# Feed-forward input, shifted by one token: built by two SyncE transfers instead of two ScalarE copies

## The chip, the cores and the metric

The kernel runs on one core of a Trainium2 chip. The metric is the device time of one execution in microseconds (us).

## What is computed

A block of four parts: attention with L2-normalised rows, a transformer of depth 6 on 8 sequences of 256 tokens by 128 features, attention with relative positions, and a mixture of 8 experts. Most of the time goes to the transformer. Each of its six layers is:

```python
def shift_tokens(t):
    a, s = jnp.split(t, 2, -1)
    s = jnp.pad(s, ((0, 0), (1, 0), (0, 0)))[:, :-1]
    return jnp.concatenate([a, s], -1)
for i in range(DEPTH):
    x = attn_layer(shift_tokens(x), Wqkv[i], q_scale[i], k_scale[i], Wo[i]) + x
    x = ffn_layer(shift_tokens(x), ln_g[i], ln_b[i], W1[i], b1[i], W2[i], b2[i]) + x
```

The shift leaves the first 64 features where they are and moves the other 64 one token later. `attn_layer` is attention in windows of 32 tokens with 16 heads of 64; `ffn_layer` is a layer norm over the features, a gated product with GELU, and a projection back.

## The kernel before, in words

The stream `Z` lies in SBUF with features on the 128 partitions and tokens on the free axis, one [128, 256] slab for each of the 8 sequences. A layer of one sequence is an item: 48 items, `t = layer * 8 + sequence`. Every engine has its own program, written out in order, and engines meet at counting semaphores. Each of them calls `step(t, ...)`, and a step has eight slots `s`. In step `t` three items are at work: item `t` has its projections, norms and rotation, item `i = t - 1` its attention, item `f = t - 2` its output projection and feed-forward part. Step `t` therefore holds the shifted input of item `t - 2`.

What happens at the start of a step, around that input:

- TensorE ends the output projection of `f` (`project_out`, L593). VectorE adds it to `Z` (`add_attention`, L1261) and raises `z1_done`.
- ScalarE, slot 0, in order: square and copy of the projection (L901, L904), two copies of a turned key block (L929, L930), then the two copies of the shifted input (L975 for the 64 features that stay, L976 for the 64 that move), a values copy (`take_values`, L915, raises `v_done`), the turned probabilities (L942). The second xf copy raises `xf_ready`.
- TensorE, slot 1, in order: projection of the next block (L512), the mean of `xf` over the features as a matmul with a constant matrix (`ln_mean_pe`, L395), which waits for `xf_ready` and `z_ready`; then the turn of the last block of item `i` (L523), its second weighing (L572), a turn of its output (L581), the variance (L401), values (L533).
- VectorE, slot 1, begins with the subtraction `xf - mean` (`ln_d_dve`, L1113, raises `ln_d`); ScalarE squares that (L854). Normalisation, norms (L1225 to L1219), the division of the weighed values (L1250, L1254) and the rotation (L1234) follow.
- `xf` is one buffer. Partition rows 64 to 127 of its token 0 are zeroed once (L1128).

SyncE issues DMAs in the order of its own program (`layer`). For item `t`: `spread_values(t, 0)`, `load_xs(t + 1)`, `spread_values(t, 1)`, `spread_values(t, 2)`, `spread_values(t, 3)`. `load_xs` makes the shifted input of the attention part by two transfers from Z (L325, L326, 64 KB and 63.8 KB). `spread_values(t, j)` waits for `v_done >= 8 t + 2 j + 2` and then issues four transfers (two for the last group) of 130 KB inside the values tile `vp` (L335). The copy that completes group 2 of item `t` is the values copy of ScalarE in slot 0 of step `t + 1`, the one right behind the two xf copies. Between these stand, at the first, second and last item of a layer, the loads of the next weights.

The waits that matter, in TensorE's slot 1 and in ScalarE's slot 0:

```python
                    if s == 1 and p2:
                        pe.wait_ge(xf_ready, f + 1)

                        pe.wait_ge(z_ready, B + f)
                        ln_mean_pe(xf[:, :], S, LN_S2 + f, bank[3])
```

Of the kernel before, what the change touches and what calls it, by code (L numbers as in the profile page):

```python
# [20 lines left out]
P = 128  # L21
B, S, DIM, H = 8, 256, 128, 16
TOK = B * S
DEPTH = 6
ITEMS = DEPTH * B
# [56 lines left out]
def build(nc, a, out):  # L82
    ctx = ExitStack()
    with ctx:
        def sb(name, shape, dt=F32):
            return ctx.enter_context(nc.sbuf_tensor(name, shape, dt))

        def sem(name):
            return ctx.enter_context(nc.semaphore(name))
# [17 lines left out]
        Z = sb("Z", [P, B, S])  # L107
# [23 lines left out]
        xf = sb("xf", [P, S])  # L131
# [109 lines left out]
        z1_done, xf_ready, ffn_in = sem("z1_done"), sem("xf_ready"), sem("ffn_in")  # L241
# [19 lines left out]
        def _(sp):  # L261
# [15 lines left out]
            def load_q(l):  # L277
                sp.dma_start(wqk[:, 0:H * DH], a["L0_ffn_Wqkv"][l, :, 0:H * DH]).then_inc(ld_q, 16)

            def load_k(l):  # L280
                sp.dma_start(wqk[:, H * DH:2 * H * DH], a["L0_ffn_Wqkv"][l, :, H * DH:2 * H * DH]).then_inc(ld_k, 16)
# [4 lines left out]
            def load_o(l):  # L286
                sp.dma_start(wo[:, :, :], a["L0_ffn_Wo"][l].rearrange("(c p) n -> p c n", p=P)).then_inc(ld_o, 16)
# [33 lines left out]
            def load_xs(t, b, odd):  # L321

                wait(sp, z_ready, t + 1)
                wait(sp, v_full, 4 * t - 4)
                sp.dma_start(xs[0:64, odd, WIN:KW], Z[0:64, b, :]).then_inc(xs_ready, 16)  # L325
                sp.dma_start(xs[64:P, odd, WIN + 1:KW], Z[64:P, b, 0:S - 1]).then_inc(xs_ready, 16)  # L326

            def spread_values(t, j):

                sp.wait_ge(v_done, 8 * t + 2 * j + 2)  # L330
                for slot, w in ((0, 2 * j), (1, 2 * j + 2)):
                    for o in range(2):
                        if w < NW:
                            rows = slice(64 * o + WIN * slot, 64 * o + WIN * slot + WIN)
                            sp.dma_start(vp[rows, w].rearrange("p q n -> p (q n)"),  # L335
                                         vp[rows, 2 * j + 1].rearrange("p q n -> p (q n)")).then_inc(v_even[w // 4], 16)

            def layer(l, first, last):
                for n in range(B):
                    t = l * B + n  # L340
                    spread_values(t, 0)
                    if n == B - 1 and not last:
                        sp.wait_ge(p_full, 8 * t + 6)
                        load_q(l + 1)
                    if n < B - 1 or not last:
                        load_xs(t + 1, (n + 1) % B, (n + 1) % 2)
                    spread_values(t, 1)
                    if n == B - 1 and not last:
                        sp.wait_ge(p_full, 8 * t + 8)
                        load_k(l + 1)  # L350
                    if n == 0 and not first:
                        sp.wait_ge(po_full, t)
                        load_o(l)
                    if n == 1 and not first:
                        sp.wait_ge(hd_full, 3 * t - 3)
                        load_w1(l)
                        sp.wait_ge(ct_full, t - 1)
                        load_w2(l)
                    spread_values(t, 2)
                    if n == B - 1 and not last:  # L360
                        sp.wait_ge(v_full, 4 * t + 4)
                        load_v(l + 1)
                    spread_values(t, 3)
# [3 lines left out]
            for l in range(1, DEPTH - 1):  # L367
                layer(l, False, False)
            layer(DEPTH - 1, False, True)

            sp.wait_ge(p_full, 8 * ITEMS)
            for k, name in ((0, "L1_attn_Wq"), (2, "L1_attn_Wk"), (4, "L1_attn_Wv")):
# [18 lines left out]
        def _(pe):  # L391
# [232 lines left out]
            def step(t, odd, p0, p1, p2, p3=True):  # L624
                i, f = t - 1, t - 2
                for s in range(8):
                    if p0:
                        projection(t, s, odd)
                    if s in (4, 5, 6) and p2:
                        hidden(f, s - 4, p1)  # L630
                    if s == 1 and p2:
                        pe.wait_ge(xf_ready, f + 1)

                        pe.wait_ge(z_ready, B + f)
                        ln_mean_pe(xf[:, :], S, LN_S2 + f, bank[3])
                    if s == 0 and p2:
                        project_out(f, 1, p1)
                    if s == 2 and p1:
                        scores(i, 2, (sh_done, 4 * i + 2), (z1_done, i))
                    if s == 6 and p0:  # L640
                        scores(t, 0, (sh_done, 4 * t), *([(h_done, 3 * f + 2)] if p2 else []))
                    if s == 7 and p0:
                        scores(t, 1, (sh_done, 4 * t - 1), *([(h_done, 3 * f + 3)] if p2 else []))
                    if s >= 2 and p0:
                        turn(t, s - 2, s)
                    if s < 2 and p1:
                        turn(i, s + 6, s, s == 1 and not p0)
                    if s == 3 and p1:

                        scores(i, 3, (ln_done, LN_S2 + i) if p2 else (sh_done, 4 * i + 1))  # L650
                    if s == 5 and p0:
                        values(t, 1, odd)
                    if s in (0, 1, 4, 5) and p1:
                        weigh(i, (0, 1, 0, 0, 2, 3)[s])
                    if s in (0, 3, 4) and p1:
                        turn_probs(i, (1, 0, 0, 2, 3)[s])
                    if s in (1, 2, 5, 6) and p1:
                        turn_out(i, (0, 0, 1, 0, 0, 2, 3)[s])
                    if s == 1 and p2:
                        ln_var_pe(S, LN_S2 + f, bank[3])  # L660
                    if s == 7 and p2:
                        contract(f, p0)
                    if s in (3, 7) and p0:
                        values(t, s // 2 - 1, odd)
                    if s == 1 and p1:
                        values(i, 3, 1 - odd)
                    if s == 2 and p2:
                        ln_wide_pe(S, LN_S2 + f, bank[3])
                    if s == 7 and p0:
                        turn_probs(t, 0)  # L670
                    if s == 7 and p1:
                        project_out(i, 0, p0)
# [178 lines left out]
        def _(act):  # L851
# [106 lines left out]
            def step(t, odd, p0, p1, p2, p3=True):  # L958
                i, f = t - 1, t - 2
                for s in range(8):  # L960
                    if p0:
                        take_raw(t, s)
                    if s == 3 and p1:
                        exps(i, 2)
                    if s == 7 and p0:
                        exps(t, 0)
                    if s >= 2 and p0:
                        take_turned(t, s - 2, s)
                    if s < 2 and p1:
                        take_turned(i, s + 6, s)  # L970
                    if s in (4, 5, 6) and p2:
                        gelu(f, s - 4)
                    if s == 0 and p2:
                        act.wait_ge(z1_done, f + 1)
                        nc.scalar.copy(xf[0:64, :], Z[0:64, f % B, :])  # L975
                        nc.scalar.copy(xf[64:P, 1:S], Z[64:P, f % B, 0:S - 1]).then_inc(xf_ready, 1)  # L976
                    if s == 1 and p2:
                        ln_sq_act(S, LN_S2 + f)
                    if s in (4, 6) and p0:
                        take_values(t, s // 2 - 2, 1)  # L980
                    if s in (0, 2) and p1:
                        take_values(i, s // 2 + 2, 1)
                    if s in (0, 3, 4) and p1:
                        take_probs(i, (1, 0, 0, 2, 3)[s])
                    if s == 7 and p0:
                        take_probs(t, 0)
                    if s in (1, 2, 5, 6) and p1:
                        take_out(i, (0, 0, 1, 0, 0, 2, 3)[s])
                    if s == 3 and p1:
                        exps(i, 3)  # L990
                    if s == 7 and p0:
                        exps(t, 1)
                    if s in (3, 5, 7) and p0:
                        take_values(t, s // 2 - 1, 0)
                    if s == 1 and p1:
                        take_values(i, 3, 0)
# [722 lines left out]
```

## Time and profile before

| | us |
|---|---|
| median of 3 runs | 2863.02 (2860.31 to 2863.55) |
| the profiled execution | 2861.27 |
| its span | 2859.5 |
| TensorE busy | 2546.6 (89%) |
| VectorE busy | 2165.9 (76%) |
| ScalarE busy | 1800.5 (63%) |
| GpSimd busy | 1551.6 (54%) |
| DMA queue q1, share of 16 engines | 18.6% |

The span runs from the first to the last instruction of the profiled execution; the time of that execution is a little longer. Names of engines in rows: PE TensorE matmul, PEld TensorE weight load, DVE VectorE, ACT ScalarE, POOL GpSimd, SPq SyncE's queue. A busy time is a sum over the whole span; a timeline or a chain of one step shows who waits for whom.

### The profile page before, as it was taken

The numbers are of one execution on the slowest core, as the hardware profiler recorded it, in microseconds if no ns is written. First come the engines' busy times: TensorE is split into PE (matmuls) and PEld (weight loads), VectorE is DVE, ScalarE is ACT, GpSimd is POOL, SyncE is SP. The second block draws the span as 40 slices with busy tenths as digits, with TensorE's granted clock in tenths as the row PEclk, the third lists the DMA queues.
The fourth block names the chain that finished last, engine by engine and source line by source line (L and its number), as shares of the span: only waits on it lengthen the run. The fifth ranks groups of instructions, "written<-read, shape, count | busy, mean of one in ns | idle before, by whom it ended". The sixth has DMA issues, their size and how long they took to land.

```text
span 2859.5 us, 60067 instructions
## 1 busy us (share of the span) xinstructions
PE 2546.6 (89%) x23054; PEld 1643.1 (57%) x23054; DVE 2165.9 (76%) x3861; ACT 1800.5 (63%) x3546; POOL 1551.6 (54%) x1315
## 2 busy tenths in 40 slices
PE   5768999999999999999999999999999788889998
PEld 3435555555555555555555555555555566666665
DVE  2359889889888888888988988988887588872233
ACT  1137777777777777777777777777776366663333
POOL 1047667667667666666766766766665222211111
PEclk8769999999999999999999999999999899998999
DMA  3002222222132222222223212222222200000000
GB/s 97 0 19 50 48 46 58 69 61 50 41 74 66 47 49 48 72 63 46 50 48 81 58 43 54 60 60 60 50 48 51 90 1 1 1 1 1 4 5 8
DMA packets 75486, 127.26 MB, mean 45 GB/s; under 512 B 24757, under 2 KB 48579, under 8 KB 75203
## 3 DMA queue, kind: packets, MB, share of 16 engines
q1 hardware_dynamic: 75202, 123.42, 18.6%
q8 instruction: 186, 3.05, 0.5%
q14 instruction: 98, 0.79, 0.1%
HBM read 26.56 MB, written 1.07 MB: 10 GB/s over the span
## 4 chain that ended last, share of the span: by engine, by line
PE 38%; DVE 37%; issue 12%; ACT 8%; POOL 4%; DMA 0%; SPq 0%; ACTq 0%; DVEq 0%; POOLq 0%
DVE work L1225 6%; DVE work L1229 6%; PE bank L593 6%; DVE n L1217 5%; PE bank L815 4%; DVE mx L1239 4%; POOL rn L1523 3%; DVE rot L1234 3%; PE bank L512 3%; DVE n2m L1219 2%; PE bank L621 2%; ACT L955 2%; PE obank L825 2%; PE bank L825 2%; PE bank L560 2%
## 5 line engine op out<-in xcount | busy, mean ns | idle before, releaser
L1523 POOL TENSOR_TENSOR rn<-n2m,cst 128x8 f32<-128x8 f32 x384 | 630.9, 1643 | 208.6 <-DVE n2m L1219 172.0
L1530 POOL TENSOR_TENSOR touch<-cst 128x1 f32<-128x1 f32 x384 | 268.4, 699 | 418.7 <-DVE work L1225 418.7
L1534 POOL TENSOR_TENSOR work<-work,tab 128x512 f32<-128x512 f32 x384 | 488.1, 1271 | 0.0
L512 PE MATMUL bank<-wqk,xs 128*128 128x512 f32 x768 | 424.6, 635 | 31.8 <-ACT kT L930 15.4
L523 PE MATMUL bank<-cst,rot 128*128 128x128 f32 x1536 | 248.5, 285 | 52.5 <-DVE rot L1234 52.5
L901 ACT ACTIVATE work<-bank 128x512 f32<-128x512 f32 x384 | 229.6, 598 | 87.1 <-PE bank L512 86.9
L1225 DVE TENSOR_TENSOR work<-rot,rn 128x512 f32<-128x512 f32 x384 | 263.3, 686 | 26.9 <-POOL rn L1523 26.3
L1538 POOL TENSOR_TENSOR lnr<-lnv,cst 128x2 f32<-128x2 f32 (+1 forms) x88 | 66.3, 753 | 392.2 <-DVE lnv L1117 392.2
L1229 DVE TENSOR_TENSOR work<-work,tab 128x512 f32<-128x512 f32 x384 | 265.8, 692 | 13.3
L523 PEld LDWEIGHTS bank<-cst,rot 128*128 128x128 f32 x1536 | 169.4, 141 | 167.0 <-DVE rot L1234 129.5
L1234 DVE TENSOR_TENSOR rot<-work 128x512 f32<-128x512 f32 x384 | 261.7, 682 | 0.4
L1217 DVE TENSOR_REDUCE n<-work 128x8 f32<-128x512 f32 x384 | 260.8, 679 | 1.2 <-ACT work L901 1.2
L915 ACT COPY vp<-lnbank 64x512 f32<-64x512 f32 x384 | 222.9, 580 | 58.0 <-PE lnbank L533 54.5
L1219 DVE TENSOR_SCALAR n2m<-n 128x8 f32<-128x8 f32 x384 | 236.7, 616 | 13.3
L904 ACT COPY rot<-bank 128x512 f32<-128x512 f32 x384 | 224.2, 584 | 0.0
L942 ACT COPY pT<-bank 128x512 f32<-128x512 f32 x192 | 112.4, 585 | 169.5 <-PE bank L560 167.2
L572 PE MATMUL obank<-vp,pT 128*32 128x130 f32 x6144 | 210.9, 277 | 0.5 <-ACT pT L942 0.5
L533 PE MATMUL lnbank<-wv,xs 128*64 128x512 f32 x768 | 208.9, 623 | 0.0
L551 PE MATMUL bank<-kT,qT 128*32 128x128 f32 x6144 | 208.4, 276 | 0.0
L512 PEld LDWEIGHTS bank<-wqk,xs 128*128 128x128 f32 x768 | 119.7, 190 | 148.4 <-issue 84.0
L551 PEld LDWEIGHTS bank<-kT,qT 128*32 128x32 f32 x6144 | 156.6, 110 | 70.2 <-issue 70.2
L572 PEld LDWEIGHTS obank<-vp,pT 128*32 128x32 f32 x6144 | 158.7, 109 | 63.3 <-ACT pT L942 38.7
(197 smaller groups left out, 4909.8 us busy)
## 6 DMA issues: line engine op xcount, KB each, us to landing
vp<-vp SPq DMA_DIRECT2D x672, 130.0 KB, 2.4
wqk<-in_L_ffn_Wqkv SPq DMA_DIRECT2D x12, 512.0 KB, 4.3
wv<-in_L_ffn_Wqkv SPq DMA_DIRECT2D x6, 512.0 KB, 3.6
wo<-in_L_ffn_Wo SPq DMA_DIRECT2D x6, 512.0 KB, 4.1
xs<-Z SPq DMA_DIRECT2D x48, 64.0 KB, 2.0
xs<-Z SPq DMA_DIRECT2D x48, 63.8 KB, 2.0
kT<-rel_by_distance SPq DMA_DIRECT2D x1, 2048.0 KB, 8.1
vp<-in_L_ffn_w SPq DMA_DIRECT2D x1, 2048.0 KB, 13.3
```

What stands on the lines that cost most here:

```text
L512: nc.tensor.matmul(bank[s % 2][:, :], xs[:, odd, WIN + r * P:WIN + r * P + P], wqk[:, lo:lo + 512], start=True, stop=True).then_inc(p_full, 1)
L523: mm = nc.tensor.transpose(bank[(s + 1) % 2][:, q * P:q * P + P], rot[:, c, q * P:q * P + P], ident)
L551: mm = nc.tensor.matmul(s[WIN * w:WIN * w + WIN, q * P:q * P + P], qT[:, 4 * g + q, lo:lo + WIN], keys if w % 2 else keys[:, :, ::-1, :], ...
L572: mm = nc.tensor.matmul(obank[WIN * w:WIN * w + WIN, q // 2, (q % 2) * VB:(q % 2) * VB + VB], pT[:, k % 2, q * P + w * WIN:q * P + w * WIN ...
L1217: red(n2[:, c % 2, :], heads(sq[:, c % 2, :]), AX, ALU.add).then_inc(n2_raw, 1)
L1219: nc.vector.tensor_scalar(n2m[:, c % 2, :], n2[:, c % 2, :], 1e-24, None, ALU.max).then_inc(n2_done, 1)
L1225: tt(heads(qn[:, c % 2, :]), heads(rot[:, c, :]), rn[:, c % 2, :].unsqueeze(2).broadcast_to([P, PAIRS, DH]), ALU.mult).then_inc(qn_done, 1)
L1229: tt(heads(t1[:, c % 2, :]), heads(qn[:, c % 2, :]), cos, ALU.mult).then_inc(t1_done, 1)
L1234: tt(rot[:, c, :], t1[:, c % 2, :], t2[:, c % 2, :], ALU.add).then_inc(rot_done, 1)
L1523: tt(rn[:, c % 2, :], n2m[:, c % 2, :], const("mhalf"), ALU.pow).then_inc(rn_done, 1)
L1530: tt(touch[:, c:c + 1], const("mhalf")[:, 0:1], const("mhalf")[:, 0:1], ALU.mult)
L1534: tt(t2[:, c % 2, :].rearrange("p (h o d) -> p h o d", o=2, d=DH // 2), swapped, sin, ALU.mult).then_inc(t2_done, 1)
```

## The change

The two copies leave ScalarE. SyncE gets `load_xf(f)`, which waits for `z1_done >= f + 1` and issues two transfers from `Z` to `xf` with the same elements as the copies, each of which adds 16 to `xf_ready`. It is called for item `t - 1` between groups 2 and 3 of the spread of item `t`, and once behind the last layer. TensorE waits for 32 per item.

```diff
+            def load_xf(f):
+                sp.wait_ge(z1_done, f + 1)
+                sp.dma_start(xf[0:64, :], Z[0:64, f % B, :]).then_inc(xf_ready, 16)
+                sp.dma_start(xf[64:P, 1:S], Z[64:P, f % B, 0:S - 1]).then_inc(xf_ready, 16)
+
             def layer(l, first, last):
...
                     spread_values(t, 2)
+                    if t >= 1:
+                        load_xf(t - 1)
...
             layer(DEPTH - 1, False, True)
+            load_xf(ITEMS - 1)
...
                     if s == 1 and p2:
-                        pe.wait_ge(xf_ready, f + 1)
+                        pe.wait_ge(xf_ready, 32 * f + 32)
...
-                    if s == 0 and p2:
-                        act.wait_ge(z1_done, f + 1)
-                        nc.scalar.copy(xf[0:64, :], Z[0:64, f % B, :])
-                        nc.scalar.copy(xf[64:P, 1:S], Z[64:P, f % B, 0:S - 1]).then_inc(xf_ready, 1)
```

SyncE's queue in the first layer, before, from group 1 to the first issues of group 3 of an item's spread:

```order
L335 DMA vp<-vp 32x1040 [waits v_done]
L335 DMA vp<-vp 32x1040 x3
L335 DMA vp<-vp 32x1040 [waits v_done]
L335 DMA vp<-vp 32x1040 x3
L335 DMA vp<-vp 32x1040 [waits v_done]
L335 DMA vp<-vp 32x1040
```

The same place in the changed kernel, from group 1 to the first issues of group 3:

```order
L335 DMA vp<-vp 32x1040 [waits v_done]
L335 DMA vp<-vp 32x1040 x3
L335 DMA vp<-vp 32x1040 [waits v_done]
L335 DMA vp<-vp 32x1040 x3
L340 DMA xf<-Z 64x256 [waits z1_done]
L341 DMA xf<-Z 64x255
L335 DMA vp<-vp 32x1040 [waits v_done]
L335 DMA vp<-vp 32x1040
```

The two new transfers stand behind the four of group 2 and ahead of the two of group 3.

ScalarE's slot 0, before (the key copies, the shifted input, the values, the probabilities):

```order
L929 COPY kT<-bank1 64x4x128 [waits t_full]
L930 COPY kT<-bank1 64x4x128
L975 COPY xf<-Z 64x256 [waits z1_done]
L976 COPY xf<-Z 64x255
L915 COPY vp<-lnbank 64x8x64 [waits v_full]
L942 COPY pT<-bank4 128x512 [waits o_full,pt_full]
```

And in the changed kernel, where the line numbers of ScalarE are 8 higher:

```order
L937 COPY kT<-bank 64x4x128 [waits t_full]
L938 COPY kT<-bank 64x4x128
L923 COPY vp<-lnbank 64x8x64 [waits v_full]
L950 COPY pT<-bank 128x512 [waits o_full,pt_full]
L909 ACTIVATE work<-bank 128x512 [waits n2_raw,p_full]
```

The values copy now follows the key copies directly. TensorE, VectorE and GpSimd keep their orders.

## Rows read from the trace of the kernel before

**Rows 1.** The page, busy time of each engine and share of the span
```profile
PE 2546.6 (89%) x23054; PEld 1643.1 (57%) x23054; DVE 2165.9 (76%) x3861; ACT 1800.5 (63%) x3546; POOL 1551.6 (54%) x1315
```

**Rows 2.** Windows: length; busy PE, PEld, DVE, ACT, POOL; granted clock, DMA share, GB/s
```profile
1016.25:1058.46 42.21, 39.21 (x402) 24.43 (x401) 36.76 (x65) 30.78 (x56) 29.16 (x25) 1.00 0.22 49
1058.46:1102.56 44.10, 40.75 (x402) 25.49 (x401) 36.86 (x65) 30.84 (x56) 29.17 (x25) 0.96 0.21 47
...
1019.10:1029.50 10.40, 9.18 (x101) 5.56 (x100) 9.67 (x18) 7.96 (x16) 7.87 (x8) 1.00 0.27 61
```

**Rows 3.** Chain of waits at a step's start: start, us, what
```profile
1018.27 0.86 PE bank L512 x2
...
1019.18 0.68 PE bank L395 x2
```

**Rows 4.** Timeline of ScalarE there: start us, us, instruction
```profile
1017.88 0.41 ACT L975 COPY xf<-Z 64x256 f32<-64x256 f32 x1
1018.30 0.40 ACT L976 COPY xf<-Z 64x255 f32<-64x255 f32 x1
1018.61 0.58 ACT L915 COPY vp<-lnbank 64x512 f32<-64x512 f32 x1
```

**Rows 5.** The tile xf: durations ns min/median/max, first/last start; who waited
```profile
L975 ACT COPY xf<-Z x48: 404/405/406, 258.4 to 2225.5; 64x256 f32<-64x256 f32 x48
L976 ACT COPY xf<-Z x48: 400/400/403, 258.8 to 2225.9; 64x255 f32<-64x255 f32 x48
...
  PEld bank L395: 41.5, 48
```

**Rows 6.** Timeline of VectorE: the addition of the attention to Z
```profile
1016.25 0.42 DVE L1261 TENSOR_TENSOR Z<-Z,bank 128x256 f32<-128x256 f32 x1 [3.48 <-PE bank L593]
```

**Rows 7.** Timeline of SyncE's queue: issues of the spread and of xs
```profile
997.51 2.42 SPq L335 DMA_DIRECT2D vp<-vp  x4
1000.03 0.54 SPq L325 DMA_DIRECT2D xs<-Z  x1
1000.61 0.60 SPq L326 DMA_DIRECT2D xs<-Z  x1
...
1019.22 1.14 SPq L335 DMA_DIRECT2D vp<-vp  x2
```

**Rows 8.** Timeline at the first item: second xs issue, matmul that waits
```profile
173.91 0.60 SPq L326 DMA_DIRECT2D xs<-Z  x1
...
176.00 0.50 PEld L512 LDWEIGHTS bank<-wqk,xs 128*128 128x128 f32 x2 [3.93 <-issue]
```

**Rows 9.** Line 326, the second xs transfer, x48: issue to landing
```profile
DMA to landing us min/median/max: 2.0/2.0/4.5
```

**Rows 10.** Line 335, the spread transfers: issue times in ns, min/median/max
```profile
L335 SPq DMA_DIRECT2D vp<-vp x672: 507/592/2166, 197.8 to 2209.1; - x168
```

**Rows 11.** Timeline of the weight loads: the mean matmul on xf
```profile
1019.14 0.30 PEld L395 LDWEIGHTS bank<-xf,cst 128*128 128x128 f32 x2 [0.84 <-ACT xf L976]
```

**Rows 12.** Timeline of VectorE and TensorE behind the mean
```profile
1019.88 0.42 DVE L1113 TENSOR_TENSOR lnd<-xf,bank 128x256 f32<-128x256 f32 x1 [0.21 <-PE bank L395]
...
1020.31 1.10 PE L572 MATMUL obank<-vp,pT 128*32 128x130 f32 x32
...
1022.85 0.19 DVE L1250 RECIPROCAL rd<-obank 128x8 f32<-128x8 f32 x1
```

**Rows 13.** Timeline of the last item's step
```profile
2225.47 0.41 ACT L975 COPY xf<-Z 64x256 f32<-64x256 f32 x1 [5.43 <-DVE Z L1261]
...
2226.34 0.30 PEld L395 LDWEIGHTS bank<-xf,cst 128*128 128x128 f32 x2 [1.76 <-ACT xf L976]
```

**Rows 14.** Timeline of TensorE late in the step from 1058.46
```profile
1091.81 0.59 PE L546 MATMUL bank<-cbf 128*128 128x512 bf16 x1 [1.60 <-DVE hT L1273]
```

**Rows 15.** A mean matmul pair at the low clock, and its stretch
```profile
2244.51 1.22 PE L395 MATMUL lnbank<-X,cst 128*128 128x256 f32 x2 [0.97 <-DVE X L1335]
...
2242.50:2245.80 3.30, 2.26 (x6) 1.24 (x6) 0.84 (x2) 0.00 (x0) 0.00 (x0) 0.50 1.08 351
```

## The prediction

> **What bounds the kernel now.** I read the page's busy times first, then one step of the feed-forward/attention pipeline, then who waits for the shifted input. TensorE is busy 89% of the span, VectorE 76%, ScalarE 63% [rows 1]. So ScalarE has the most room of the three. An average hides where it matters, so the step comes next. The program runs 48 items, one step each. A step lasts 42.21 us, and inside it TensorE is busy 39.21 us and ScalarE 30.78 us [rows 2]. Between the first and the last of the 48 copies the mean step is (2225.5 - 258.4) / 47 = 41.85 us [rows 5]; the last one, without a projection, is short. Work taken off ScalarE brings something only where ScalarE is what the others wait for.
>
> At the copies to be removed it is not. The chain of waits through the start of a step goes from a projection matmul on TensorE (0.86 us from 1018.27) straight to the mean matmul that reads xf, at 1019.18 [rows 3]; the copies are not on it. The copies run beside that projection. One is 0.41 us and begins at 1017.88, the other 0.40 us at 1018.30, and ScalarE goes on to the values at 1018.61 [rows 4]. They end at 1018.70, while TensorE is busy with the projection until 1018.27 + 0.86 = 1019.13. So the copies finish 0.4 us early. The table of the tile xf lists 41.5 us for which weight loads waited for ScalarE's second copy [rows 5], 0.86 us each. That is a trap. It is idle time of the weight-load side only, while the array itself was still multiplying, and it costs nothing in a full step. The slack of 0.4 us is what the change has to live with.
>
> **What the change removes.** 96 copies, 48 x (0.404 + 0.400) = 38.6 us of ScalarE time [rows 5]. Cover: TensorE's projection hides them, so I cost the removal at no gain by itself. If it did reach the end it would be worth 0.73 us a step, the time by which the values copy moves forward (1018.61 to 1017.88) [rows 4].
>
> **What it adds.** Two transfers of SyncE per item. Their place in SyncE's queue counts more than their size. They stand behind the third group of spread transfers (four issues), which waits for v_done, that is for the values copy at 1018.61. The wait for z1_done costs nothing in a full step: the addition to Z starts at 1016.25 and takes 0.42 us [rows 6], well before SyncE arrives. Step by step, for the step that starts at 1016.25:
> - The values copy starts at 1017.88 instead of 1018.61, since nothing stands before it. From its start to SyncE's first issue it now takes 1019.22 - 1018.61 = 0.61 us [rows 4, 7]. So the spread starts at 1018.49.
> - Four spread issues and then two transfers out of Z already stand back to back elsewhere in each step: 997.51, then 1000.03 and 1000.61 [rows 7]. So four issues take 2.52 us and the first of the two takes 0.58 us. The first xf issue is at 1021.01, the second at 1021.59.
> - From the second issue to the waiting matmul: the xs transfers have the same source and size. At the very first item TensorE waits for them alone: issue 173.91, weight load 176.00, 2.09 us [rows 8]. That is the value I take. Landing alone is 2.0 us median and at most 4.5 us, for xs transfers that mostly follow spreads too [rows 9]. So the bounds are 2.0 and 4.5 us. I take the value near the lower end because the median lies there.
> - The weight load for the mean starts at 1021.59 + 2.09 = 1023.68 instead of 1019.14 [rows 11]: **+4.54 us** per full step.
>
> By the fit in the Trainium skill, "SBUF — State Buffer", section "The DMA setup-cost knee", a 64 KB transfer takes an estimated 2.15 us, where the trace has 2.0 us of landing; by it the sum would be 0.15 x 48 = 7 us higher. The page says itself that its fit overstates mid sizes, and the sum goes by the trace.
>
> **Who stands behind the wait.** TensorE executes in order. Behind the mean matmul are the last turn of the item before, its second weighing, the turn of the output and the variance. VectorE's order has the subtraction from xf ahead of the next normalisation. It comes to it with only 0.21 us to spare [rows 12]: it has no backlog with which to fill 4.5 us. GpSimd waits for VectorE's norms, ScalarE for TensorE's turns. So all stop and start again together, and the stop adds its full length. After it little can be caught up. Over 1019.10 to 1029.50 TensorE is busy 9.18 of 10.40 us and VectorE 9.67 us [rows 2], so at most 1.22 us of waits is there to vanish. ScalarE's lead of 0.73 us helps nobody, since VectorE paces this stretch. I take no recovery and keep 1.22 us for the range.
>
> The third spread group is not delayed. The fourth comes after the two new issues, but it waits for a values copy two slots later anyway, and that copy is now later too. Its receiver, the third weighing, is in slot 4. Weight transfers in SyncE's queue at the layers' first, second and last item are issued before or after, and their reader is a step away. The last item has no projection before its mean, and its second copy is awaited for real. Its z1_done comes at 2225.47, when ScalarE starts; 0.58 + 2.09 after that is 2228.14 instead of 2226.34 [rows 13]: +1.80 us.
>
> **The clock.** A new stop of TensorE of about 4.5 us (1019.13 to 1023.68) appears in each step. In the step from 1058.46 TensorE stopped 1.60 us for hT [rows 14]. That step has a mean granted clock of 0.96, so part of it ran at 1.2 GHz, and is 44.10 us long, 1.89 us more than its neighbour at 1.00 [rows 2]. After a stop almost three times that, I expect the drop to be the rule. Its price depends on what runs slowly. Right behind the stop the mean matmul pair takes 1.22 us at 1.2 GHz instead of 0.68 us [rows 3, 15], and VectorE waits for it: +0.54 us. What follows has a cover. Weighing starts at 1020.31 and takes 1.10 us, so it ends at 1021.41, but VectorE reads its result only at 1022.85 [rows 12]. So 1.44 us is free, about what turn and weighing lose at half speed (0.66 + 1.10 more). I take 0.54 us, with 0 and 1.89 us as ends.
>
> The Trainium skill, "TensorE: Matmul & The Clock Gate", section "HAM oscillation — how this bites in real kernels", speaks against this change: a wait for a DMA between groups of matmuls makes each next group start at the low clock, every time round. By that rule the low clock comes in all 47 steps; without it the sum would be 25 us lower.
>
> **The sum** against the profiled execution (2861.27 us; its span is 2859.5 us): 47 x 4.54 = 213.4; last item 1.8; clock 47 x 0.54 = 25.4; together +240.6, so 3101.9 us. The median of the runs shown is 1.75 us above the profiled one, which gives 3103.6. I say **3103 us**, +8.4%. Some spread issues take far longer than 0.59 us (up to 2.17) [rows 10]; where the last of the four does, it adds to the stop. I leave that to the range.
>
> **The rivals.**
> - *The low clock reaches a stretch paced by TensorE* and costs the whole 1.89 us per step instead of 0.54. For: it did so in the one step that shows it [rows 2]. Against: that was at the end of a step, not behind the mean. 47 x (4.54 + 1.89) + 1.8 = 304, so 3165 us. [...] 17%.
> - *The stop is partly caught up*: the 1.22 us of later waits vanish and no clock drops. 47 x (4.54 - 1.22) + 1.8 = 158, so 3019 us. For: the trace does not show the pipeline with a stop there. Against: VectorE has 0.73 us of idle time in that stretch. 9%.
> - *The transfers queue behind the spreads*: landing 4.5 us instead of 2.0 adds 2.5 x 48 = 120 us, so 3221 us. For: the maximum of the row [rows 9]. Against: its median, in the same neighbourhood. 5%.
> - *Faster*: the transfers land before TensorE needs them, and ScalarE's 0.73 us per step reaches the end. It decides at 1019.14: a landing before that. Then 2861.3 - 48 x 0.73 = 2826 us. It would need the second issue by 1017.05, before the values copy even starts, while the order of the queue puts it behind that copy and four issues. 2%.
> - *Nothing happens*: landing in the same slack, ScalarE never awaited; 2863 us. The same reason against. 1%.
>
> **How the numbers follow.** Main case 66%, with 3076 (no clock drop) to about 3125 for its own spread; rivals 17, 9, 5, 2 and 1%. The range of 3060 to 3165 us takes in the main case, the price of the heavier clock and half of the way to the caught-up case. It leaves out the far part of that one, the queued landing, and both cases without a slowdown. For this kernel a measurement tells about 0.2% (6 us) from no change. Chances: faster 0.02, same 0.01, slower 0.97.
>
> **What would show it.** Per step: a length near 47.3 us; the weight load for xf waiting some 4.5 us for SyncE's transfer; SyncE's row with four vp issues and then xf at about 4.8 us after the addition to Z; a granted clock of 0.5 behind the stop in most steps; ScalarE's busy time 38.6 us lower. The prediction is wrong if the step stays within 2 us of 42.21, if the xf issues stand before the spread, or if VectorE works on during TensorE's stop.

## The result, and the profile after

The change makes the kernel slower. The median is 3127.74 us (3127.29 to 3132.70, 4 runs) against 2861.92 us for the kernel before: a ratio of 1.0933, 95% interval 1.0914 to 1.0952. That is 266 us more, where the forecast's sum had 241. The profiled execution took 3132.70 us, with a span of 3130.9 us. Line numbers of the engines' programs are 4 to 8 higher than before.

The page, with busy time of each engine and share of the span, answers to [rows 1]; below it the chain's shares by engine, which were 38% PE, 37% DVE and 12% issue before:

```profile
PE 2665.2 (85%) x23054; PEld 1733.2 (55%) x23054; DVE 2149.0 (69%) x3861; ACT 1773.3 (57%) x3450; POOL 1553.9 (50%) x1315
...
PE 42%; DVE 28%; issue 11%; ACT 10%; SPq 5%; DMA 3%; POOL 1%; ACTq 0%; POOLq 0%; DVEq 0%
```

ScalarE has 96 instructions less and 27 us less of busy time, not the forecast's 38.6. Busy time counts two overlapping instructions once: the durations of all its instructions fell by 36.8 us in sum, and 9.6 us of overlap are gone with them. TensorE has the same instructions and 119 us more of busy time: they ran at a lower clock. SyncE's queue and the DMA had under 0.5% of the chain each before and have 8% together now.

Who waited for whom, from the table of waits (total, times, longest):

```profile
PEld bank L403 <- DMA xf<-Z: 253.4, 48, 6.7
DVE lnd L1117 <- PE bank L403: 241.9, 48, 6.5
PE bank L403 <- DMA xf<-Z: 214.7, 48, 5.8
```

TensorE's array stood 214.7 us over 48 items for the transfer: 4.47 us each. Its weight loads show 253.4 us, which is 0.81 us more of each wait. That is idle time beside a running projection, as the 0.86 us before were. VectorE waits for the mean behind it.

One step on the chain of waits (start, us, what); the addition to Z in it starts at 449.48:

```profile
450.51 0.58 ACT kT L938
451.09 0.50 ACT vp L923
...
451.61 0.51 SPq L335
...
454.06 0.59 SPq L340
...
454.69 2.01 DMA xf<-Z
...
456.74 1.22 PE bank L403 x2
457.96 0.85 PE bank L531 x4
458.82 1.89 PE obank L580 x32
```

This is the forecast's sequence: values copy, four spread issues, two xf issues, landing. The second xf issue comes 5.21 us after the start of the addition, and the weight load at 456.74 comes 7.26 us after it. Before, it came at 1019.14 - 1016.25 = 2.89 us. VectorE had nothing else to do. Its timeline in the same step (brackets: idle before):

```profile
452.21 0.68 DVE L1238 TENSOR_TENSOR rot<-work 128x512 f32<-128x512 f32 x1
458.00 0.42 DVE L1117 TENSOR_TENSOR lnd<-xf,bank 128x256 f32<-128x256 f32 x1 [5.11 <-PE bank L403]
...
460.98 0.20 DVE L1254 RECIPROCAL rd<-obank 128x8 f32<-128x8 f32 x1
```

In place of 0.21 us [rows 12] it stands idle 5.11 us.

Further on in the same step, and at the same place of the step from 496.94, VectorE's norm of the next block:

```profile
465.06 0.69 DVE L1221 TENSOR_REDUCE n<-work 128x8 f32<-128x512 f32 x1 [0.76 <-ACT work L909]
...
514.29 0.69 DVE L1221 TENSOR_REDUCE n<-work 128x8 f32<-128x512 f32 x1 [2.49 <-ACT work L909]
```

It waits for ScalarE's square of the next projection (L909). Over all 384 norms this wait has 52.4 us, and 1.2 us before.

Three steps in a row, by windows (columns as in [rows 2]; the eighth figure is the granted clock), and then the stretches of two of them in which the clock was low:

```profile
402.80:449.50 46.70, 40.47 (x403) 25.60 (x402) 36.45 (x66) 30.22 (x54) 29.20 (x25) 0.96 0.21 47
449.50:496.90 47.40, 41.23 (x402) 26.24 (x401) 36.32 (x65) 30.21 (x54) 29.20 (x25) 0.93 0.21 46
496.90:546.20 49.30, 43.08 (x404) 26.80 (x402) 36.41 (x66) 30.21 (x54) 29.20 (x25) 0.90 0.27 66
...
410.90:414.30 3.40, 3.40 (x41) 2.55 (x40) 3.30 (x7) 1.58 (x3) 2.21 (x3) 0.50 0.00 0
...
503.10:513.30 10.20, 9.05 (x52) 5.39 (x53) 5.88 (x11) 2.75 (x5) 6.15 (x6) 0.50 0.04 9
```

The stop is the same in all three (7.26 to 7.32 us from the addition to the weight load), but the steps last 46.7, 47.4 and 49.3 us. They differ in how long the 1.2 GHz lasts behind the stop: 3.4, 6.8 and 10.2 us. All of the first 46 steps are of these three kinds. A full step without any clock loss would last 42.2 + the stop. That is the measure here (e4_warm below shows it). By the starts of L1265 and L403 in the first 46 steps, 11 steps have the short low stretch and cost 0.05 us more than that, 23 the middle one with 0.87 us, 12 the long one with 2.68 us. Sum: 46 x 4.47 = 206 us for the stops and 53 us for the clock.

Taken directly, these 46 steps grew by 256.2 us, from 1943.0 to 2199.2; it is 3 less than 259 because the steps before were not all 42.2 us long. The two profiled executions differ by 271 us. The 47th step and the last item add 5.5 and 1.7 us. 2.7 us lie ahead of the first addition to Z (259.5 against 256.8 us) and 5.3 us behind the last item. Those 8 us I don't assign: in the traces of the experiments the first addition starts at 255.9 to 258.5 us, and the time behind the last one is 635.4 to 643.7 us, against 634.5 before and 641.5 in the change.

### The profile page after: what moved, and what is told of

Read it like the earlier page. It is cut to its first block, busy times and chain, and to the rows that moved or that the text cites. A ratio compares the mean times of both kernels' runs of the same rounds, so it can differ in the third digit from the quotient of the medians.

```text
span 3130.9 us, 60067 instructions
## 1 busy us (share of the span) xinstructions
PE 2665.2 (85%) x23054; PEld 1733.2 (55%) x23054; DVE 2149.0 (69%) x3861; ACT 1773.3 (57%) x3450; POOL 1553.9 (50%) x1315
## 3 DMA queue, kind: packets, MB, share of 16 engines
q8 instruction: 186, 3.05, 0.4%
## 4 chain that ended last, share of the span: by engine, by line
PE 42%; DVE 28%; issue 11%; ACT 10%; SPq 5%; DMA 3%; POOL 1%; ACTq 0%; POOLq 0%; DVEq 0%
PE bank L601 5%; DVE n L1221 4%; PE bank L823 4%; SPq L335 4%; PE lnbank L541 3%; DVE work L1229 3%; DVE work L1233 3%; PE bank L520 3%; DVE mx L1243 3%; DMA xf<-Z 3%; DVE rot L1238 3%; PE obank L580 3%; PE bank L531 3%; PE bank L629 2%; ACT L963 2%
## 5 line engine op out<-in xcount | busy, mean ns | idle before, releaser
L520 PE MATMUL bank<-wqk,xs 128*128 128x512 f32 x768 | 435.5, 650 | 32.5 <-ACT kT L938 16.1
L1221 DVE TENSOR_REDUCE n<-work 128x8 f32<-128x512 f32 x384 | 261.1, 680 | 52.4 <-ACT work L909 52.4
L909 ACT ACTIVATE work<-bank 128x512 f32<-128x512 f32 x384 | 229.5, 598 | 108.3 <-PE bank L520 108.0
L937 ACT COPY kT<-bank 64x512 f32<-64x512 f32 x192 | 112.2, 584 | 304.7 <-PE bank L531 304.7
L531 PE MATMUL bank<-cst,rot 128*128 128x128 f32 x1536 | 263.9, 298 | 12.0 <-DVE rot L1238 11.9
L531 PEld LDWEIGHTS bank<-cst,rot 128*128 128x128 f32 x1536 | 187.1, 150 | 121.4 <-DVE rot L1238 72.7
L580 PE MATMUL obank<-vp,pT 128*32 128x130 f32 x6144 | 251.0, 312 | 0.5 <-ACT pT L950 0.5
L403 PE MATMUL bank<-xf,cst 128*128 128x256 f32 x96 | 52.3, 643 | 214.7 <-DMA xf<-Z 214.7
L580 PEld LDWEIGHTS obank<-vp,pT 128*32 128x32 f32 x6144 | 184.3, 123 | 76.8 <-ACT pT L950 38.6
L1223 DVE TENSOR_SCALAR n2m<-n 128x8 f32<-128x8 f32 x384 | 214.8, 559 | 13.3
L541 PE MATMUL lnbank<-wv,xs 128*64 128x512 f32 x768 | 219.9, 652 | 0.0
```

The lines of the kernel that those rows point to most:

```text
L520: nc.tensor.matmul(bank[s % 2][:, :], xs[:, odd, WIN + r * P:WIN + r * P + P], wqk[:, lo:lo + 512], start=True, stop=True).then_inc(p_full, 1)
L531: mm = nc.tensor.transpose(bank[(s + 1) % 2][:, q * P:q * P + P], rot[:, c, q * P:q * P + P], ident)
L541: mm = nc.tensor.matmul(vbank[64 * o:64 * o + 64, :], xs[:, odd, (2 * w + 1) * WIN:(2 * w + 3) * WIN], wv[:, :].rearrange("p (a o d) -> p ...
L580: mm = nc.tensor.matmul(obank[WIN * w:WIN * w + WIN, q // 2, (q % 2) * VB:(q % 2) * VB + VB], pT[:, k % 2, q * P + w * WIN:q * P + w * WIN ...
L909: nc.scalar.activation(sq[:, s % 2, :], bank[s % 2][:, :], ACT.Square).then_inc(sq_done, 1)
L1221: red(n2[:, c % 2, :], heads(sq[:, c % 2, :]), AX, ALU.add).then_inc(n2_raw, 1)
```

## The experiments

Each time stands beside runs of the kernel before on the same chip.

**e1_ahead.** The change, with the two transfers ahead of the spread in SyncE's queue:

```diff
-                    spread_values(t, 2)
                     if t >= 1:
                         load_xf(t - 1)
+                    spread_values(t, 2)
```

> The two xf transfers stand ahead of the second group of the spread in SyncE's queue instead of behind it. My theory (the cost is the place in the queue plus the landing time): the first issue comes 0.45 us after the addition to Z starts, the second some 0.6 us later, and the mean's weight load 2.1 us after that, near 3.1 us, against 2.89 us before the change. So the stop falls from 4.4 to about 0.2 us a step, no clock drop, and the time is 2862 + 47 x 0.2 = 2871 us (2863 to 2880). Rival (a transfer between SBUF tiles is too slow whatever its place, or it is slowed by the spreads): at least 2.5 us a step is left, 2980 us or more.

Measured: 2888.41 us against 2861.87, ratio 1.0091 (1.0077 to 1.0105). Of 266 us only 27 are left. Chain of waits in an ordinary step, whose addition to Z starts at 427.78:

```profile
428.23 0.50 SPq L340
...
428.77 2.01 DMA xf<-Z
...
430.82 0.71 PE bank L403 x2
```

The landing takes the same 2.01 us as in the change, and the weight load starts 0.15 to 0.19 us later than before the change instead of 4.4 us. So the same transfers with the same bytes cost a tenth of the loss in another place. The first issue comes 0.45 us after the addition instead of 4.58: 1.68 us of that were the wait for the values copy and 2.45 us the four issues. The time is 17 us above the expectation. Five steps, the first of each new layer, were 2.2 to 2.8 us longer. SyncE's timeline at one of them, and the chain of waits:

```profile
555.06 0.38 SPq L287 DMA_DIRECT2D wo<-in_L_ffn_Wo  x1
555.52 0.56 SPq L340 DMA_DIRECT2D xf<-Z  x1
556.12 0.59 SPq L341 DMA_DIRECT2D xf<-Z  x1
...
556.12 4.17 DMA xf<-Z
```

The 512 KB of Wo leave 1.06 us ahead of the second xf transfer, and that one lands after 4.17 us instead of 2.01.

**e2_two_issues.** The transfers in the middle of the spread's four issues:

```diff
                 for slot, w in ((0, 2 * j), (1, 2 * j + 2)):
+                    if slot == 1 and f >= 0:
+                        load_xf(f)
                     for o in range(2):
...
-                    spread_values(t, 2)
-                    if t >= 1:
-                        load_xf(t - 1)
+                    spread_values(t, 2, t - 1)
```

> The two xf transfers stand in the middle of the second group of the spread: two issues ahead of them instead of four. Place theory: 1.27 us earlier than in the change, so a stop of 4.42 - 1.27 = 3.15 us and 47 x 3.15 = 148 us for the stops, 3010 us without any clock loss. If the clock falls there as it does in the change (about 1.2 us a step) 3066 us. Rival (only the landing counts, not the issues ahead): no change from 3128 us.

Measured: 3039.75 us, ratio 1.0632 (1.0616 to 1.0648). The mean's weight load waits until 495.02 in the step whose addition starts at 489.02, so its stop is 6.00 - 2.89 = 3.11 us, and 3.14 us in the mean of the steps, as expected. The time lies between the two sums, 3010 and 3066. Two steps show why:

```profile
489.00:534.30 45.30, 39.13 (x402) 24.50 (x401) 36.74 (x65) 30.28 (x54) 29.16 (x25) 1.00 0.29 72
348.70:396.80 48.10, 43.16 (x403) 26.81 (x402) 36.39 (x66) 30.17 (x54) 29.15 (x25) 0.89 0.21 45
```

After the shorter stop the clock does not always fall. In 14 of 46 steps it stays at 2.4 GHz, in 23 there is one low stretch of 3.4 us, and nine have more.

These 23 show what the place of a low stretch is worth, measured against the same step before plus its stop. Six begin up to 0.4 us ahead of the mean's weight load and cost 0.42 to 0.54 us. Six begin 0.2 us behind it and cost 0.35 to 0.42 us. Eleven begin 0.6 us or more behind it and cost nothing (0.02 us at most).

**e3_no_copies.** The kernel before, without the copies and without the wait for them:

```diff
-                        pe.wait_ge(xf_ready, f + 1)
...
-                    if s == 0 and p2:
-                        act.wait_ge(z1_done, f + 1)
-                        nc.scalar.copy(xf[0:64, :], Z[0:64, f % B, :])
-                        nc.scalar.copy(xf[64:P, 1:S], Z[64:P, f % B, 0:S - 1]).then_inc(xf_ready, 1)
```

> The kernel before without the two copies and without the wait for them: xf stays all zeros, so the shifted input of the feed-forward part is left out. It shows what taking the copies off ScalarE is worth at most. My theory (TensorE's projection hides them): 2862 us, within 6 us. Rival (ScalarE's 0.73 us reaches the end): 2862 - 47 x 0.73 = 2828 us.

Measured: 2864.85 us against 2861.87, ratio 1.0007 (0.9998 to 1.0015). The copies are worth nothing. By windows, from one addition to Z to the next, its step is

```profile
1014.96:1057.14 42.18, 39.26 (x402) 24.45 (x401) 36.74 (x66) 30.29 (x54) 29.16 (x25) 1.00 0.22 49
```

against the 42.21 us of [rows 2], with 30.29 us of ScalarE instead of 30.78. With the rest of the program as it is, no way of making xf can gain more than this.

**e4_warm.** The change, with TensorE kept busy during the stop. The matmuls are on constants and the mean overwrites their result:

```diff
-                        pe.wait_ge(xf_ready, 32 * f + 32)
-
                         pe.wait_ge(z_ready, B + f)
+                        for _n in range(5):
+                            nc.tensor.matmul(bank[3][:, :], onesm, const("rot")[:, 0:512], start=True, stop=True)
+                        pe.wait_ge(xf_ready, 32 * f + 32)
```

> The change, with five matmuls of 512 columns on constants ahead of TensorE's wait for xf (their result is overwritten): TensorE is busy for about 4.3 of the 4.4 us of the stop. The wait for the transfer stays. Theory (the rest of the loss over the stops is the clock): no low clock in the steps, every step 42.2 + 4.4 = 46.6 us, the time 2862 + 47 x 4.42 + 2 = 3072 us. Rival (the rest is something else, such as the lost lead of ScalarE or a slower DMA): 3128 us stays.

Measured: 3078.69 us, ratio 1.0758 (1.0744 to 1.0773). TensorE's timeline, and the step by windows:

```profile
447.47 4.56 PE L642 MATMUL bank<-cst 128*128 128x512 f32 x10
451.92 0.70 PE L403 MATMUL bank<-xf,cst 128*128 128x256 f32 x2
...
444.60:491.20 46.60, 43.55 (x412) 26.31 (x411) 36.73 (x65) 30.29 (x54) 29.15 (x25) 1.00 0.21 47
```

The mean starts where it starts in the change, 7.3 us after the addition, and the first 46 steps last 42.2 us plus the stop, to 0.01 us in the mean. Adding work that nobody needs made the kernel 49 us faster than the change, 3127.74 to 3078.69. That is the clock's part. The other 217 us (3078.69 - 2861.87) are those of the stops: 46 x 4.47 = 206 us, and 8 us at the last two items.

**e5_wo_behind.** As e1_ahead, and the load of Wo is issued behind the xf transfers:

```diff
-                    if n == 0 and not first:
-                        sp.wait_ge(po_full, t)
-                        load_o(l)
...
                     if t >= 1:
                         load_xf(t - 1)
+                    if n == 0 and not first:
+                        sp.wait_ge(po_full, t)
+                        load_o(l)
                     spread_values(t, 2)
```

> As e1_ahead, and at the first item of each layer the 512 KB load of Wo is issued behind the two xf transfers instead of just ahead of them. In e1_ahead exactly those five steps were 2.2 to 2.8 us longer, their xf transfer landing 4.2 us after its issue. Theory (the big transfer ahead in the queue delays the small one): the five steps are as short as the others, 42.4 us; 2888 - 5 x 2.4 = 2876 us, and 2 to 4 less without the clock drops behind those stops, so 2873 us. Rival (those steps are long for another reason, such as new weights being read): 2888 us stays.

Measured: 2875.22 us against 2861.97, ratio 1.0047 (1.0033 to 1.0061). The five steps now have 42.4 to 43.1 us instead of 44.6 to 45.2, so the Wo transfer ahead was their cause. What is left is mainly the 0.15 to 0.19 us in each step.

**e6_half_each.** As e5_wo_behind, with the half that stays copied by ScalarE:

```diff
-                sp.dma_start(xf[0:64, :], Z[0:64, f % B, :]).then_inc(xf_ready, 16)
-                sp.dma_start(xf[64:P, 1:S], Z[64:P, f % B, 0:S - 1]).then_inc(xf_ready, 16)
+                sp.dma_start(xf[64:P, 1:S], Z[64:P, f % B, 0:S - 1]).then_inc(xf_moved, 16)
...
-                        pe.wait_ge(xf_ready, 32 * f + 32)
+                        pe.wait_ge(xf_ready, f + 1)
+                        pe.wait_ge(xf_moved, 16 * f + 16)
...
+                    if s == 0 and p2:
+                        act.wait_ge(z1_done, f + 1)
+                        nc.scalar.copy(xf[0:64, :], Z[0:64, f % B, :]).then_inc(xf_ready, 1)
```

> As e5_wo_behind, with the half that is not shifted copied by ScalarE again, at its old place, and only the shifted half by a transfer of SyncE. One issue instead of two: it starts 0.45 us after the addition to Z starts and lands 2.1 us later, at about 2.6 us, and the copy ends at 2.1 us; TensorE needs xf at 2.89 us. Theory (only what arrives after 2.89 us costs): no stop at all, 2862 us like the kernel before, within 6 us. Rival (a transfer costs more than its lateness, by disturbing others or by SyncE's issues): 2870 us or more.

Measured: 2871.51 us, ratio 1.0037 (1.0024 to 1.0049). The expectation failed by its own bound: the rival's 2870 us came. The timeline of SyncE and of the weight load, in a step whose addition starts at 1062.55:

```profile
1063.00 0.50 SPq L340 DMA_DIRECT2D xf<-Z  x1
...
1065.59 0.30 PEld L402 LDWEIGHTS bank<-xf,cst 128*128 128x128 f32 x2 [1.00 <-issue]
```

The transfer was there 1.9 us after its issue, at about 1064.9, and the copy was done at 1064.59. The mean began at 1065.59 all the same, 3.04 us after the addition, and the row blames no transfer but "issue". Something other than the data held it.

**e7_act_queue.** The kernel before, with the copies replaced in place by DMAs that ScalarE issues:

```diff
-                        pe.wait_ge(xf_ready, f + 1)
+                        pe.wait_ge(xf_ready, 32 * f + 32)
...
-                        nc.scalar.copy(xf[0:64, :], Z[0:64, f % B, :])
-                        nc.scalar.copy(xf[64:P, 1:S], Z[64:P, f % B, 0:S - 1]).then_inc(xf_ready, 1)
+                        act.dma_start(xf[0:64, :], Z[0:64, f % B, :]).then_inc(xf_ready, 16)
+                        act.dma_start(xf[64:P, 1:S], Z[64:P, f % B, 0:S - 1]).then_inc(xf_ready, 16)
```

> The kernel before, with the two copies replaced in place by two DMAs that ScalarE issues itself, so that no spread stands ahead of them in a queue. ScalarE comes to them 1.63 us after the addition to Z starts; with 0.6 us an issue the second starts at 2.2 us, lands at 4.3 us. Theory (place in the order of the issuing engine, plus landing): a stop of 1.4 us per step, 2862 + 47 x 1.4 = 2928 us, and little of the clock loss of the change. Rival (the number of transfers, not the issuing queue, makes the cost): near 3128 us.

Measured: 2885.61 us, ratio 1.0083 (1.0070 to 1.0097), 42 us better than expected. Timeline of ScalarE and of its issues; the addition starts at 1027.29:

```profile
1027.72 0.58 ACT L929 COPY kT<-bank 64x512 f32<-64x512 f32 x1 [1.09 <-PE bank L523]
1027.74 0.47 ACTq L975 DMA_DIRECT2D xf<-Z  x1
1028.24 0.61 ACTq L976 DMA_DIRECT2D xf<-Z  x1
1028.31 0.58 ACT L930 COPY kT<-bank 64x512 f32<-64x512 f32 x1
```

The issues do not queue behind the two key copies that stand ahead of them in the program: the first starts beside L929 and the second 0.07 us ahead of L930. They start 0.45 us after the addition, as in e1_ahead, and the time is that of e1_ahead. The five long steps are there too (44.6 to 45.5 us), with Wo on SyncE's queue and xf on ScalarE's, and one of 43.9 us besides.

**e8_one_wait.** As e6_half_each, with one semaphore for both halves:

```diff
-                sp.dma_start(xf[64:P, 1:S], Z[64:P, f % B, 0:S - 1]).then_inc(xf_moved, 16)
+                sp.dma_start(xf[64:P, 1:S], Z[64:P, f % B, 0:S - 1]).then_inc(xf_ready, 16)
...
-                        pe.wait_ge(xf_ready, f + 1)
-                        pe.wait_ge(xf_moved, 16 * f + 16)
+                        pe.wait_ge(xf_ready, 17 * f + 17)
```

> As e6_half_each, but the copy and the transfer raise the same semaphore (1 and 16), so TensorE waits once instead of twice for xf. In e6_half_each the mean began at 3.05 us after the addition to Z in nearly every full step, against 2.89 us before the change, though both halves of xf were there by 2.4 us. Theory (TensorE's fourth wait ahead of the mean costs 0.16 us): the mean begins at 2.89 us again, steps of 42.2 us, 2862 us. Rival (the DMA half itself is what delays it, or the semaphore raised by a DMA is seen later): 3.05 us and 2871 us stay.

**e9_extra_wait.** The kernel before, with a wait that is always met:

```diff
                         pe.wait_ge(xf_ready, f + 1)
+                        pe.wait_ge(z1_done, f + 1)
```

> The kernel before, with one more wait of TensorE ahead of the mean, for a count that has been reached long before (z1_done). Nothing else is changed, no DMA is added. Theory (a wait costs its own 0.16 us there): 2862 + 47 x 0.16 = 2870 us, the mean at 3.05 us. Rival (a wait that is already met is free): 2862 us.

Measured, against 2864.14 us: e8_one_wait 2866.73 us, ratio 1.0007 (0.9998 to 1.0015); e9_extra_wait 2874.53 us, ratio 1.0031 (1.0019 to 1.0043). The weight load ahead of the mean, of e8_one_wait (its addition at 1017.79):

```profile
1020.68 0.30 PEld L402 LDWEIGHTS bank<-xf,cst 128*128 128x128 f32 x2 [0.84 <-ACT xf L982]
```

and of e9_extra_wait (its addition at 976.78):

```profile
979.82 0.30 PEld L395 LDWEIGHTS bank<-xf,cst 128*128 128x128 f32 x2 [1.00 <-ACT xf L977]
```

2.89 us with three waits and a DMA, 3.04 us with four waits and no DMA. A fourth wait costs 0.15 us a step there, even when it is met: the first 46 steps of e9_extra_wait are 7.5 us longer in sum and those of e6_half_each 6.4 us. The rest of their 10.4 and 9.5 us is not in these steps; the intervals of the ratios reach down to 5.4 and 6.9 us. A transfer that arrives in time costs nothing: e8_one_wait ties with the kernel before. Nothing here beats the kernel before, and by e3_no_copies nothing of this kind could.

## Why the prediction was right, and where a term was off

- **The removal brings nothing.** Shown by e3_no_copies. The trap of the 41.5 us [rows 5] was one: e3_no_copies has neither the copies nor that wait and gains nothing.
- **The stop of 4.54 us.** The sum of values copy, four issues, two issues and 2.09 us gave a weight load 7.43 us after the addition. It came at 7.26 to 7.32, so 4.42 us in an ordinary step and 4.47 in the mean. The values copy was done a little sooner than reckoned: SyncE's first issue came at 2.13 us and not at 2.24. The four issues took 2.45 us and not 2.52. From the second xf issue to the weight load it was 2.09 us in the median, the value taken; its landing, the term with the widest bounds, has a median of 2.0 us, the lower bound. The mean is 0.05 us higher because in four steps a spread issue took longer and put off the xf issue by 0.2 to 1.4 us, which the prediction left to its range. e2_two_issues confirms that each issue ahead costs its 0.6 us: two fewer shorten the stop by 1.28 us.
- **Nothing is caught up.** Right. In e4_warm the steps are 42.2 us plus the stop to 0.01 us, and VectorE's 5.11 us of idle time fill the stop.
- **The clock: mechanism right in kind, size off.** The drop came in all 46 steps, as the step on the clock expected. Its term, "47 x 0.54", was mis-sized: 53 us in the profiled execution and 49 us by e4_warm, about 1.1 us a step. That is what 3103 us lacks: the stops' term was 3 us too high and the clock's 28 us too low. The term priced the mean pair alone, "What follows has a cover". The pair did cost 0.52 us in the middle steps (1.26 us from weight load to subtraction, 0.74 before), and a low stretch of 3.4 us over the pair costs that and no more (e2_two_issues). But the low clock lasted 6.8 us in 23 steps and 10.2 us in 12, past the weighing, and reached the values and the next projection. There VectorE waits at its next norm, which brings a step to 0.87 and to 2.68 us, more than the 1.89 us of the bound from [rows 2]. In the other direction, in the 11 steps with the short stretch the mean pair still runs at full speed (0.70 us at 410.14) and weighing and turn have their cover, so nothing is lost. The heavier rival (3165 us) and the main case both hold a part of the truth. That the free case of 11 steps and the heavy one of 12 partly cancel in the time is luck.
- **The last item** cost as reckoned in kind: its load came 3.05 us after the addition, against 2226.34 - 2225.02 = 1.32 before, +1.7 us where 1.8 stood.
- **Queued landing.** In this change it did not happen: the longest landing of xf is 2.3 us. A landing of 4 us was real in e1_ahead and e7_act_queue, behind Wo and not behind the spreads.

The Trainium skill's rule on waits for a DMA between matmul groups ("TensorE: Matmul & The Clock Gate", section "HAM oscillation — how this bites in real kernels") is that the next group starts at the low clock, every time round. The trace after agrees in part: each of the 46 steps has a low stretch (granted clock 0.90 to 0.96, against 1.00 in 45 of the same 46 before), but in 11 of them the pair right behind the wait still ran at full speed. In e2_two_issues, with 3.14 us of stop, 14 of 46 steps kept the full clock.

What stays open: why the same stop is followed by a low stretch of 3.4 us in one step and 10.2 us in another, and why it begins 0.5 to 2.1 us ahead of the mean's weight load in 35 steps and 0.8 us behind it in 11. The traces show what each costs, but no run sets the length or the start by itself.

## What to carry to other kernels

Before moving a copy to a DMA, write down the moment its reader needs the data and count from its source: wait, issues that stand ahead in that queue, its own issues at 0.6 us each, 2.0 us of landing. Here the data came 4.8 us later than the copies had brought it, against 0.4 us of slack, while the engine relieved had no part in the path. If the transfer must be made, it belongs ahead of the bulk issues and ahead of any large transfer released at the same time; and a stop of TensorE is to be priced with the clock behind it, which was 49 us on top of 217 us.

## What the runs showed that was not expected

- A DMA issued by ScalarE started 0.45 us after its condition was met, beside ScalarE's own key copy and ahead of another that stands earlier in the program (e7_act_queue).
- A fourth wait of TensorE ahead of one matmul, already met, delayed it by 0.15 us, 7.5 us over the first 46 steps; the median was 2874.53 us against 2864.14 (e9_extra_wait).
- A 64 KB transfer behind a 512 KB one landed after 4.17 us instead of 2.01 us, and issuing it from another engine's queue did not help (e1_ahead, e7_act_queue).
- Useless matmuls in a stop of TensorE gave back 49 us (e4_warm).
- A low stretch of TensorE's clock of the same 3.4 us costs half a microsecond over the mean pair and nothing 0.6 us behind its start (e2_two_issues).
